# A transformer block on one core: the opening in another order (loads, transposes, statistics, fills)

## What is computed

```python
h = _layernorm(x, ln1_g, ln1_b)
x = _attention(h, h, sa_wq, sa_wk, sa_wv, sa_wo, sa_bo) + x
h = _layernorm(x, ln2_g, ln2_b)
x = _attention(h, cond_emb, ca_wq, ca_wk, ca_wv, ca_wo, ca_bo) + x
h = _layernorm(x, ln3_g, ln3_b)
p = h @ ff_w1 + ff_b1
a, gate = (p[..., :D_FF], p[..., D_FF:])
h = a * jax.nn.gelu(gate, approximate=False) @ ff_w2 + ff_b2
return h + x
```

## Time and profile before

| What | Value |
|---|---|
| Median of 3 runs | 1222.76 us (1222.62 to 1223.83) |
| Profiled execution | 1222.66 us |
| Its span in the profile | 1220.6 us |
| TensorE busy | 1186.3 us, 97% of the span |
| VectorE, GpSimd, ScalarE busy | 767.2, 743.0, 642.3 us |
| Chain that ended last, by engine | TensorE 89%, GpSimd 4%, ScalarE 2%, VectorE 2% |

### The profile page before, as it was taken

How to read it: one execution, slowest core, us unless ns; L and a number is a source line. 1 busy time by engine, 2 the same in 40 slices (tenths; PEclk the granted TensorE clock), 3 DMA queues, 4 the chain that set the end, 5 groups by cost and what they waited for, 6 DMA issues and landing times.

```text
span 1220.6 us, 23620 instructions
## 1 busy us (share of the span) xinstructions
PE 1186.3 (97%) x9385; PEld 776.6 (64%) x9385; DVE 767.2 (63%) x1289; ACT 642.3 (53%) x954; POOL 743.0 (61%) x381
## 2 busy tenths in 40 slices
PE   3899999999999999999999999999999999999998
PEld 3655665566566656666655664666666666678887
DVE  4757566575575576675665756458777877674433
ACT  3447554445445446744544454557855586536432
POOL 1196787886876976877877768864556346321000
PEclk9899999999999999999999999999999999999999
DMA  3010000000000000000000000011111110010000
GB/s 111 14 27 10 6 17 16 5 11 23 6 10 23 6 10 23 6 10 14 14 11 12 10 13 6 23 31 50 48 40 32 33 33 14 15 36 18 18 18 18
DMA packets 63539, 25.76 MB, mean 21 GB/s; under 512 B 34551, under 2 KB 61383, under 8 KB 63431
## 3 DMA queue, kind: packets, MB, share of 16 engines
q1 hardware_dynamic: 63375, 24.25, 7.6%
q10 hardware_dynamic: 56, 0.01, 0.0%
HBM read 21.62 MB, written 2.10 MB: 19 GB/s over the span
## 4 chain that ended last, share of the span: by engine, by line
PE 89%; POOL 4%; ACT 2%; DVE 2%; issue 1%; DMA 1%; SPq 0%; DVEq 0%; POOLq 0%; ACTq 0%
PE psum L858 22%; PE psum L844 22%; PE psum L736 15%; PE psum L721 9%; PE psum L881 7%; PE psum L821 6%; POOL acc L1402 4%; PE psum L941 4%; PE psum L869 3%; PE psum L826 2%; PE psum L895 1%; ACT probs L1273 1%; DVE xr L1084 1%; DMA probs<-in_ctx 1%; DVE m_part L1047 1%
## 5 line engine op out<-in xcount | busy, mean ns | idle before, releaser
L1402 POOL TENSOR_TENSOR acc<-acc,probs 128x1024 f32<-128x1024 f32 x192 | 458.7, 2389 | 70.1 <-ACT probs L1273 49.7
L1273 ACT ACTIVATE probs<-psum 128x1024 f32<-128x1024 f32 (+1 forms) x320 | 317.1, 1031 | 275.6 <-PE psum L844 271.1
L1047 DVE TENSOR_REDUCE m_part<-psum 128x2 f32<-128x1024 f32 x256 | 308.9, 1222 | 223.0 <-PE psum L821 223.0
L858 PE MATMUL psum<-probs,val 128*64 128x512 f32 x1024 | 244.9, 603 | 0.0
L1402 POOL TENSOR_TENSOR acc<-probs 128x1024 f32<-128x1024 f32 (+1 forms) x64 | 152.8, 2388 | 142.2 <-ACT probs L1273 120.3
L1084 DVE SCALAR_TENSOR_TENSOR xr<-psum,d_cols,xr 128x256 f32<-128x256 f32 x512 | 207.8, 476 | 35.1 <-PE psum L881 34.6
L858 PEld LDWEIGHTS psum<-probs,val 128*64 128x64 f32 x1024 | 63.3, 136 | 113.7 <-issue 98.8
L844 PE MATMUL psum<-row_max,minus 64*128 64x512 f32 (+1 forms) x640 | 125.9, 389 | 0.0
L844 PE MATMUL psum<-q_hi,k_hi 64*128 64x512 f32 x512 | 101.6, 393 | 0.3 <-DVE m_part L1047 0.3
L844 PE MATMUL psum<-q_lo,k_hi 64*128 64x512 f32 x512 | 100.8, 389 | 0.0
L844 PE MATMUL psum<-q_hi,k_lo 64*128 64x512 f32 x512 | 100.8, 389 | 0.0
(11 more groups left out here) (147 smaller groups left out, 2132.1 us busy)
## 6 DMA issues: line engine op xcount, KB each, us to landing
xr<-in_x SPq DMA_DIRECT2D x8, 256.0 KB, 5.8
wv_raw<-in_L_xattn_sa_wv SPq DMA_DIRECT2D x8, 256.0 KB, 2.9
wqk_raw<-in_L_xattn_sa_wq SPq DMA_DIRECT2D x16, 128.0 KB, 2.5
wqk_raw<-in_L_xattn_sa_wk SPq DMA_DIRECT2D x16, 128.0 KB, 2.3
wo_raw<-in_L_xattn_sa_wo SPq DMA_DIRECT2D x16, 128.0 KB, 2.4
d_cols<-d_rows SPq DMA_DIRECT2D x128, 2.0 KB, 2.1
wqk_raw<-in_L_xattn_ca_wq SPq DMA_DIRECT2D x16, 128.0 KB, 2.6
probs<-in_L_xattn_ff_w SPq DMA_DIRECT2D x8, 256.0 KB, 3.4
```

The source lines that it names most:

```text
L858: mm = pe.matmul(psum[d, PVB + half, :], values(J)[0:plan.ks, kt, own], probs[buffer_of(J, u)][0:plan.ks, h, :], start=(kt == 0), stop=(kt ...
L1047: dve.tensor_reduce(m_part[:, half, :, t, kh], psum[:, bank0:bank0 + 2, :], AX.X, ALU.max).then_inc(s_x_read, 1)
L1273: act.activation(probs[buffer_of(J, u)][0:plan.ks, :, :], psum[0:plan.ks, bank0:bank0 + 2, :], ACT.Exp, scale=SCALE).then_inc(s_exp, 1)
L1402: pool.tensor_tensor(total, last if kt == 1 else total, now, ALU.add).then_inc(s_acc, 1)
```

## The change

Only the order of the words changes, in the table `OPENING`; no instruction is added or dropped. (The other tables are only wrapped in another way.) SyncE: the second half's rows x1 are loaded right behind x0, then the query and key weights, then the value weights; the context and the rest follow as before. TensorE: the vectors' transpose is first, then those of the rows; the context's first transposes come behind the first turns of keys and queries, `K0` and `Q0`. VectorE: the copy of the vectors stands behind the first centring, the second half's statistics and centring follow ahead of all residues of h, and the context's residue comes behind these. ScalarE: the second root is ahead of the first affine pass; the query and key weights are split behind the first half's affine passes, the value weights behind the second half's, then comes the context's copy. GpSimd: the fills are first, then the weights' residues.

The opening's words as far as they differ, before (-) and after (+):

```diff
 OPENING = {
-    "sp": "x0@-240.63 G+@-211.64 W+@-157.08 x1@-144.11 c@-110.87 x2@-48.90 x3@-27.69 G+++@-15.98 W++@0.55 "
+    "sp": "x0@-240.63 x1@-230.00 W+@-225.00 G+@-222.00 c@-110.87 x2@-48.90 x3@-27.69 G+++@-15.98 W++@0.55
...
-    "pe": "c0+@-198.21 v@-160.08 t0.0+@-150.33 t0.1+@-141.80 t1.0+@-103.87 t1.1+@-85.45 K0+@-83.67 Q0+@-79.47 "
-            "K1+@-76.82 Q1+@-59.30 X0+@-51.69
+    "pe": "v@-205.00 t0.0+@-150.33 t0.1+@-141.80 t1.0+@-103.87 t1.1+@-85.45 K0+@-83.67 Q0+@-79.47 c0+@-78.00
+            K1+@-76.82 Q1+@-59.30 X0+@-51.69
...
-    "dve": "n0+@-200.50 z0+@-152.41 v@-130.55 n1+@-125.91 c0+@-125.76 z1+@-103.87 l0.0+@-98.72 l0.1+@-81.19 "
-            "l1.0+@-59.64 l1.1+@-56.18 K0+@-53.98
+    "dve": "n0+@-200.50 z0+@-152.41 v@-150.00 n1+@-140.00 z1+@-103.87 l0.0+@-98.72 l0.1+@-81.19
+            l1.0+@-59.64 l1.1+@-56.18 c0+@-55.00 K0+@-53.98
...
-    "act": "s0+@-205.50 G+@-202.70 c0+@-105.80 a0.0+@-69.91 s1+@-56.59 W+@-48.50 a0.1+@-45.76 a1.0+@-43.56 "
-            "a1.1+@-32.77 K0+@-31.46
+    "act": "s0+@-205.50 s1+@-150.00 a0.0+@-69.91 a0.1+@-45.76 W+@-45.00 a1.0+@-43.56
+            a1.1+@-32.77 G+@-32.00 c0+@-31.80 K0+@-31.46
...
-    "pool": "W+@-186.55 f@-44.93 G+@-41.34 W++@-41.16 b0+@84.77 b1+@97.72",
+    "pool": "f@-200.00 W+@-186.00 G+@-41.34 W++@-41.16 b0+@84.77 b1+@97.72",
 }
```

More of the change, by code:

```diff
@@ L134 @@
     "sp": "T-@53.60 G+++@54.97 W+++@55.81 O@56.20 M0+@67.01",
[L135 to L141, removed]
[3 rows of a table added]
     "pool": "W++@-10.47 G++@-3.63 A1@0.29 A3@1.63 O@4.09",
@@ L182 @@
     "sp": "G16.0@-95.65 W16.0@-47.08 W17.0@17.87 M16.0@88.21 T15.0@98.81",
[L183 to L190, removed]
[3 rows of a table added]
     "pool": "W16.0@-24.21 G16.0@3.27 W17.0@26.42 O15.0@28.14 W18.0@39.07",
```

## The result

The changed kernel takes 1217.11 us in the median of 5 runs (1216.55 to 1217.80), against 1223.04 for the kernel before in 5 runs (1222.62 to 1223.83). The ratio is 0.9952, with a 95% interval from 0.9941 to 0.9963: 5.9 us, or 0.5%, faster. The profiled execution took 1216.59 us with a span of 1214.5, 6.1 us less than before on both counts (1222.66 and 1220.6). The prediction was 1216.3, in a range from 1214.5 to 1218.9, and faster by more than 0.2%.

The account below looks back on a forecast made before the run. The bound was the first projection's start at 24.05 us, behind waits in the opening. Gaining 6.85 us there, less 0.48 for the context's transposes, gave 6.4 us: 1222.66 becomes 1216.3, range 1214.5 to 1218.9.

Parts of the forecast that it names:

- What bounds: Opening: the first projection's start, 24.05 us, decides; TensorE waits for the context until 10.57, and the second centring takes 4.18.
- Vectors: TensorE's first transpose: last semaphore at 6.2 us, transpose done at 6.6, hidden behind the first centring ending at 7.34.
- Loads: SyncE: both halves' rows land by about 6.3 us; weight loads slip to at latest 8.9 and cost nothing.
- (c): Rival, opening: second rows land 1.4 us late or the centring still stalls by 2.8; up to 1219.1; chance 0.05.
- Fills: GpSimd: fills move to about 1.5 to 4.3 us; delay to the first statistics taken as 0, bound 0.75.
- ScalarE's chain: ScalarE bounds the middle, from the second root at 9.31 us; first projection at 17.2 instead of 24.05, 6.85 gained.
- The context on TensorE's path: Context's first transposes between the projections cost 0.48 us, or 0.72 at the low clock, nothing in a bubble.
- The clock: TensorE's slow stretches, at the first projections and between 31.8 and 45 us, assumed to keep their length against the work.
- Rival (a): First projections: clock rises later against the work, all 48 at the first pace, 2.0 us more, 1218.3; chance 0.10.
- (d): Rival: gain lost before 60 us, if GpSimd's add at 60.51 starts at a fixed time; 1222.7; chance 0.06.
- (b): Rival: clock does not fall in the row maxima, value projections save 1.5 us, 1214.8; chance 0.06.
- (e): Rival: TensorE's clock stays low after the row maxima into the first scores; slower, 1225.3 with 18 us more; chance 0.03.

Follow-up runs that it names:

- b_context_late: Kernel before with only the context's first transposes moved behind K0 and Q0 on TensorE, copy and residue likewise: 1220.72 us (ratio 0.9976).
- a_split_early: a_context_in_gap with ScalarE splitting the query and key weights ahead of the second root: 1215.70 us (ratio 0.9940 to the kernel before).
- a_loads_back: Changed kernel with the loads in the old order, second half's rows behind the value, query and key weights: 1218.41 us (ratio 0.9962 to the kernel before).
- a_fills_back: Changed kernel with the fills back behind the weights' split on GpSimd: 1217.60 us (ratio 0.9951 to the kernel before).
- a_fills_beside: a_split_early with the fills behind the weights' residue on GpSimd, beside the second centring: 1216.79 us (ratio 0.9950 to the kernel before).
- a_context_in_gap: Changed kernel with the context's first transposes between the last rows' transposes and K0, where TensorE idles: 1215.85 us (ratio 0.9941 to the kernel before).

## Why the prediction was right

By its own steps:

- **What bounds.** Confirmed. The context's transposes at the head of TensorE's queue, the second rows' landing, and the stall of the centring are three causes in a row. One at a time in the old kernel the edits bring 3.0, 0 and 1.0 us at the first projection, and all together 7.35. Most of the rest is what b_context_late's rows still show, the wait for rows and the stall. No run has ScalarE's new order (the root ahead of the affine passes, the splits later) or VectorE's copy of the vectors in their new places alone, nor the context put back in the changed kernel, so no part of the gain is measured as theirs.
- **Vectors.** Their landing was put too early: 6.2 us in the text, 6.74 to 7.60 in the ten kernels with the vectors first. In the profiled execution it stayed hidden behind the first centring, by 0.2 us; that was luck, as in five others it held the second statistics up (by 0.33 us in a_split_early).
- **Loads.** The second rows were there before the second statistics asked at 7.28, with no wait. Undone, the order costs 1.95 us at the first projection. The text's worst case for late rows, in (c), was 1.4 us: it took the old landing of the second load as half a us behind 8.35, but in a_loads_back it landed at 9.88.
- **VectorE.** Statistics at 7.28 for the forecast 7.45, centring 1.38 us for 1.38, its end at 11.05 for 11.23.
- **Fills.** Right that the centring would meet no GpSimd work. The text had 2.8 us of the gain "from the stall that goes", and either of two moves clears it once the statistics are early: with the split late, the fills can be late (a_fills_back, 1.38 us), and with the fills early, the split can be early (a_split_early, 1.38); only early split and late fills together stall (a_fills_beside, 2.73). The first statistics took 1.41 us as before, so the value taken, 0, was right. But it was hardly put to the test: the two large fills were over at 3.26, before the statistics began at 3.49, and only the small fills of `minus`, to 3.91, lay beside them.
- **ScalarE's chain.** The term mis-sized. From the second root's start to the first projection the text had 17.20 - 9.31 = 7.89 us and the trace has 16.70 - 9.13 = 7.57. The last piece, from the affine pass behind the split to the projection, is 3.90 us in both; the 0.32 lie ahead of it. It added full durations, but the starts overlap: the first affine pass starts at 9.33, while the root of 9.13 takes 0.30, and the split of 12.28 is followed by the pass at 12.80 and not at 12.90. With the 0.18 us by which everything before was early this is the whole difference between 7.35 gained and 6.85 forecast.
- **The context on TensorE's path.** Forecast 0.48, measured 0.57 in the length of the projections with the clock's rise at the same place; in a_context_in_gap the context is off the chain.
- **The clock.** The sum assumed that both slow stretches keep their length against the work. In the profiled pair they did: the lead at the first exponentials (6.8) is what the first projection (7.35) and the context (0.57) leave. That the rise came 3.98 us after the first projection in both was luck. Rival (a) is no alternative case with a chance of 0.10 but a spread between executions, 4.33 to 5.49 us for the same 24 projections. The Trainium skill (TensorE: Matmul & The Clock Gate, Part 1), cited there, says that the number of slow matmuls at a start differs from run to run: the traces agree, with 12, 18 and 24 of 24.
- **What was left out.** The claim that the lead of 6.4 us at 97 would be kept. It was 6.8 at 97 and 6.1 at the end of the span, as the bank rotation costs 0.8 us at the turn to the feed-forward part. The step that failed is "their copy and residue run while ScalarE and VectorE wait": the context's move was costed by its instructions, DMAs and queues, and not by the PSUM banks that TensorE's order hands out. That the profiled execution came within 0.3 us of the forecast is largely two errors that cancel: 0.5 us too little at the front, 0.8 too much at the back. The median lies 0.8 us from it, also because the profiled execution is 0.5 us below the median of the changed kernel's five runs; the text had put that difference at 0.1.

Rival (c) is refuted by the 1.38 us, (d) by the lead at 97, and (b) and (e) by the mean granted clock of 0.74 from 25.0 to 38.2 and 1.00 behind it, as before.

## What to carry to other kernels

In an opening with several waits in a row, undo each part in the changed kernel as well as trying each alone in the old one: at the first projection the load order here is worth nothing alone and 2 us in combination, the fills' order 1 us alone and nothing in combination. When an item moves in a queue whose order also hands out buffers round-robin, look at who inherits which buffer at the far end, where the rotation meets fixed ones. And place work that waits for a small late load (the copy of the vectors) or that another engine needs later (the split of the weights) into a wait that exists anyway, not ahead of the chain.

## What the runs showed that was not expected

- A move in the first 25 us costs 0.76 us over 1000 us later, with no instruction added, and the profile calls that idle time "issue", since it finds no releaser. The kernel's own table of who used a bank last names the wait, and another rotation in the same order takes it away.
- A centring (tensor_scalar with both tensors in SBUF) that takes 1.38 us takes 2.73 beside fills alone, 3.27 beside residues alone, and 4.18 beside both, with one or two of its four instructions held and the others at their usual 0.4. Batch statistics did not suffer beside GpSimd's residue (in a_split_early 1.40 us, two of the four wholly beside it), nor did the residues of h from PSUM, 0.69 beside the large fills in a_fills_back. Statistics beside large fills are in no run.
- The small loads of the vectors, 14 KB in seven DMAs, release TensorE at 6.74 to 7.60 us in the kernels with the vectors first: later than the half megabyte of the first rows, which the statistics have by 4.84 at the latest, and uncertain by 0.9 us.
- The pace of TensorE changes at moments not tied to the work: 4.33 to 5.49 us for the same 24 projections. With the first projection's own start, 16.70 to 17.43 us in the kernels whose opening the changed kernel shares up to there, it could account for the 1.25 us by which the changed kernel's runs differ; only profiled executions show it, so that is an estimate. What decides the moment stays open; no run was made for it.
